# Attention among the tokens: the copy of the mixes ahead of the tile's exponential on ACT, and the division of the tokens ahead of the tile's shift on DVE

## The reference, cut to what matters

```python
slice_weights = softmax((x_mid @ W_slice + b_slice) / temp, axis=-1)
slice_norm  = slice_weights.sum(axis=2)
slice_token = einsum('bhnc,bhng->bhgc', fx_mid, slice_weights)
slice_token = slice_token / (slice_norm[..., None] + 1e-05)        # token_norm
q, k, v = slice_token @ W_q, slice_token @ W_k, slice_token @ W_v
attn = softmax(einsum('bhgc,bhkc->bhgk', q, k) * SCALE, axis=-1)
out_slice = einsum('bhgk,bhkc->bhgc', attn, v)                     # mixes
out_x = einsum('bhgc,bhng->bhnc', out_slice, slice_weights)        # product
return out_x @ W_out + b_out
```

## Time and profile before

| | us |
|---|---|
| median of 3 runs | 3429.57 (3427.73 to 3431.83) |
| the profiled execution, its own time | 3429.93 |
| span of its instructions | 3428.1 |
| PE busy in the span | 3002.8 (88%) |
| DVE, ACT, POOL busy | 2535.4, 2168.8, 1989.1 |

### The profile page before, as it was taken

The page is one execution under the profiler, slowest core; times in us unless marked ns, Lnnn a source line. Parts: engine busy times, 40 slices in busy tenths (PEclk is TensorE's granted clock), DMA queues, the critical chain, the costliest instruction groups (busy, mean ns, idle before and its releaser), DMA issues. The chain is left out here.

```text
span 3428.1 us, 66757 instructions
## 1 busy us (share of the span) xinstructions
PE 3002.8 (88%) x24922; PEld 1681.2 (49%) x24922; DVE 2535.4 (74%) x3280; ACT 2168.8 (63%) x3082; POOL 1989.1 (58%) x1191
## 2 busy tenths in 40 slices
PE   8999999969898888974699758899999999999997
PEld 6777777735555555542244323344444444444444
DVE  7888888868888888872487447776767777777773
ACT  5666666658777777751244346676766666666662
POOL 7777777712788888886100256565656565655531
PEclk9999999989999999995899879999999999999999
DMA  1111111111212212111444311111111111111102
GB/s 45 39 39 40 39 39 39 35 53 44 62 55 68 58 52 58 53 40 38 156 150 150 114 36 34 32 52 45 52 46 51 46 51 46 51 47 47 48 26 52
DMA packets 208262, 191.09 MB, mean 56 GB/s; under 512 B 76381, under 2 KB 163398, under 8 KB 207562
## 3 DMA queue, kind: packets, MB, share of 16 engines
q1 hardware_dynamic: 173850, 142.95, 14.2%
q0 software_dynamic: 25600, 26.01, 3.0%
q10 hardware_dynamic: 8496, 17.87, 1.4%
HBM read 99.08 MB, written 87.65 MB: 54 GB/s over the span
## 5 line engine op out<-in xcount | busy, mean ns | idle before, releaser
L2363 POOL TENSOR_TENSOR E_w<-E_w,E_rs 128x1024 f32<-128x1024 f32 x200 | 409.0, 2045 | 528.6 <-DVE E_rs L2271 528.6
L2356 POOL DMA_INDIRECT E_row<-yb,P_gi x400 | 391.1, 978 | 399.2 <-POOLq L93 305.4
L647 POOL DMA_INDIRECT xb<-B_yt,P_gi x400 | 523.3, 1308 | 120.8 <-issue 114.1
L203 POOL TENSOR_TENSOR A_kmask<-A_ksb,A_pack_a 128x3584 f32<-128x3584 f32 x56 | 356.5, 6365 | 151.1 <-ACT A_ksb L350 151.1
L2256 DVE TENSOR_REDUCE E_mx<-E_lg 128x16 f32<-128x1024 f32 x200 | 242.3, 1211 | 203.5 <-PE E_lg L1919 198.7
L2155 ACT ACTIVATE E_w<-E_w 128x1024 f32<-128x1024 f32 x200 | 211.5, 1057 | 281.8 <-DVE E_w L2264 238.4
L2268 DVE TENSOR_REDUCE E_sm<-E_w 128x16 f32<-128x1024 f32 x200 | 243.8, 1219 | 121.4 <-ACT E_w L2155 110.2
L1950 PEld LDWEIGHTS E_wt<-S_pack_f,E_w 128*128 128x128 f32 (+1 forms) x1600 | 173.1, 143 | 198.6 <-issue 136.3
L432 DVE COPY A_vbd<-A_v 128x512 f32<-128x512 f32 x392 | 248.6, 680 | 15.2 <-PE A_v L290 15.0
L1950 PE MATMUL E_wt<-S_pack_f,E_w 128*128 128x128 f32 (+1 forms) x1600 | 220.9, 282 | 38.5 <-ACT E_mo L2203 25.9
L2264 DVE TENSOR_TENSOR E_w<-E_lg,E_mx 128x1024 f32<-128x1024 f32 x200 | 244.8, 1224 | 6.7
(11 more groups left out here) (322 smaller groups left out, 6972.3 us busy)
## 6 DMA issues: line engine op xcount, KB each, us to landing
R_xs<-xb SPq DMA_DIRECT2D x57, 256.0 KB, 2.7
yb<-R_ys SPq DMA_DIRECT2D x57, 256.0 KB, 2.0
B_x<-h SPq DMA_DIRECT2D x25, 512.0 KB
h<-B_hh SPq DMA_DIRECT2D x25, 512.0 KB
A_xg<-in_xw SPq DMA_DIRECT2D x56, 224.0 KB, 2.9
h<-A_res ACTq DMA_DIRECT2D x56, 224.0 KB, 2.0
E_hx<-h SPq DMA_DIRECT2D x48, 256.0 KB
out<-E_ob SPq DMA_DIRECT2D x96, 128.0 KB
```

Of the source, the lines that this page charges most:

```text
L203: nc.gpsimd.tensor_tensor(kmask[i % 2][:], bc(ksb[i % 2][:].unsqueeze(2), [128, J, H, Q]), bc(head_of_row[:].unsqueeze(1).unsqueeze(3), [1 ...
L647: pool.indirect_dma_start(out=xb, out_offset=bass.IndirectOffsetOnAxis(ap=routed.gi[0:k, c, b:b + 1], axis=0), in_=yt[c % LT][0:k, D * row ...
L2356: pool.indirect_dma_start(out=row[b % LR][:, k, i], out_offset=None, in_=yb, in_offset=bass.IndirectOffsetOnAxis(ap=idx[:, c, 2 * n + i:2 ...
L2363: TT(w3, w3, bc(rs[g % 3][:].unsqueeze(2), [128, 2 * SH, G]), ALU.mult).then_inc(w_done, 1)
```

## The change

On ACT the copy of the mixes moves from behind the exponential, the roots and the table load to a place ahead of the exponential. On DVE the division of the tokens moves from behind the tile's shift to a place between `highest` and `shift`. No instruction is added or removed, and the waits go with the instructions.

```diff
@@ ACT
                     if t == 0 and logs:
                         at_block(log_in, s - 1)
                         at_block(log_out, s - 3)
+                    if step == 4:
+                        act.wait_ge(mo_done, n + 1)
+                        after(act, o_done, C * n)
+                        A(mo[:].rearrange("p b q d -> p (b q d)"), WT[:, BANK[1]], ACT.Copy).then_inc(moc_done, 1)
                     if 0 <= u < TILES:
                         exponential(u)
...
                     elif step == 3:
                         act.wait_ge(asub_done, n + 1)
                         A(at, at, ACT.Exp, scale=D ** -0.5).then_inc(aexp_done, 1)
-                    elif step == 4:
-                        act.wait_ge(mo_done, n + 1)
-                        after(act, o_done, C * n)
-                        A(mo[:].rearrange("p b q d -> p (b q d)"), WT[:, BANK[1]], ACT.Copy).then_inc(moc_done, 1)
@@ DVE
                     if 0 <= u < TILES:
                         highest(u)
+                    if step == 1:
+                        token_norm(n)
                     if begins(k) and width(k) == 1:
                         leave(k)
                     if 0 <= u < TILES:
                         shift(u)
                     if begins(k) and width(k) == 2:
                         leave(k)
-                    if step == 1:
-                        token_norm(n)
-                    elif step == 3:
+                    if step == 3:
                         scores_shift(n)
```

## The result

The changed kernel takes 3396.29 us, median of 4 runs (3393.99 to 3400.89), and the kernel before took 3428.65 us, median of 4 runs with it on the same chip. The ratio is 0.991, with a 95% interval of 0.9898 to 0.9922: faster, and by more than the 0.2% that a measurement can tell. The forecast was 3399 us, in a range of 3391 to 3413. The profiled execution of the changed kernel took 3396.83 us, 33.1 us less than that of before.

What follows compares the result with a forecast made beforehand. PE was taken to set the pace in the last part, so its idle time counts. The copy's -38.1 and the division's +7.0 us sum to -31.1, from 3429.9 to 3399 us; range 3391 to 3413.

Steps and rivals of the forecast that it cites:

- The copy of the mixes: ACT, step 4: `turn_w`'s wait of 25.9 us and 13.6 us of half clock go, 1.4 come back: -38.1 us.
- the half clock: PE, step 4, `turn_w` to `product`: clock low behind the wait; 13.6 us come back if PE doesn't stand still.
- pair 0 had its full wait and ran at 1.00: Step 4: argument against the rival that the low clock comes from the work and not the wait.
- the kind of work: Rival, step 4: transposes and 64 by 64 matmuls keep the clock low, 13.6 us stay: 3412 us; chance 0.10.
- `product`'s new wait for `leave`: PE behind step 4's `turn_w`: 0.23 us a pair in six pairs, 1.4 us given back.
- ACT did not become the bound: Rival behind step 4: `inputs` waits for `hold`, gaining 25.6 us in all there: 3411 us; chance 0.07.
- The division of the tokens: DVE, step 1: division ahead of the shift makes the shift 1.29 us late in pair 1; a loss of 7.0 us.
- The term of +7.0 us: Steps 1 and 2, seven pairs: late shift delays ACT's `keep_turned`, so PE waits at `turn_tokens`; 0.96 us in pair 1.
- The waits are split otherwise than forecast: PE, steps 1 and 2: some 0.7 us at `turn_rows`, some 1 at `turn_tokens`, none at `turn_w` for the division.
- strict FIFO order: ACT, DVE and GPSIMD don't run past a waiting instruction: the division edit costs 7.0 us; without the rule, gains 8.3.
- the things that would show it wrong: Clock of 0.5 in step 4, 1 or 2; `inputs` waiting for `hold`; or pairs 1 to 6 not some 5 us shorter.
- The forecast of 31.1 us: Whole kernel: gain from both edits, -38.1 + 7.0 us, to 3399 us; chance 0.72.

Runs made afterwards that it cites:

- the ACT edit alone: Against the kernel before, only the copy of the mixes moved ahead of the exponential, DVE as before: ratio 0.9896, 167.11 us a pair.
- the second profile of before: The unchanged kernel before, profiled once more: 1243.0 us from `tokens` of pair 0 to the end; median on this chip 3427.89 us.
- the copy behind the exponential: Against the kernel before, the copy of the mixes right behind the exponential, ahead of roots and table load, DVE as before: ratio 0.9915.
- the DVE edit with the roots first: Against the kernel before, division ahead of the shift, and in step 1 ACT's roots and table load ahead of the exponential: ratio 1.0006.
- the second execution: The changed kernel run and profiled once more, on another chip, against the kernel before: ratio 0.9924, 168.12 us a pair.
- the second one mended, and `leave` ahead: Against before: mixes' copy first, `leave` behind the exponential; step 1 weighing, division, then shift, with roots and table load ahead of the exponential: ratio 0.9874.
- the DVE edit alone: Against the kernel before, only the division of the tokens moved ahead of the shift, ACT as before: ratio 1.0047.
- the kernel with `leave` ahead: Against before, the copy of the mixes first and, in step 4, `leave` right behind the exponential, DVE as before: 3386.06 us, 166.78 a pair.

## Why the prediction was right

**The copy of the mixes.** Right, in mechanism and size. All of the wait of 25.9 us went and the half clock with it; 38.1 us were forecast and 38.7 measured in the ACT edit alone. One argument was luck: that pair 0 had its full wait and ran at 1.00 holds for that one execution. In the second profile of before the same place has the same wait, and the half clock behind it:

```profile
2215.90 1.97 PE L1950 MATMUL E_wt<-S_pack_f,E_w 128*128 128x128 f32 x8 [3.42 <-ACT E_mo L2203]
```

```profile
2215.90:2221.80 5.90, 5.90 (x17) 3.25 (x17) 0.56 (x1) 2.46 (x4) 2.75 (x3) 0.53 0.05 11
```

What rules out the kind of work is the copy behind the exponential, and the half clock costs 14.5 us in the seven pairs of that execution, where the prediction had 13.6.

`product`'s new wait for `leave` is 0.40 us and not 0.23, in five pairs and not in six: the 3.84 us in brackets are counted from the end that the profile models for PE's last matmul ahead of `turn_w`, and without the wait `turn_w` begins 0.17 us sooner than that (1.10 us behind the mixes' end, where 5.11 less 3.84 is 1.27), so PE arrives sooner at `product` and waits there for the difference. `inputs` did not wait for `hold`, so ACT did not become the bound.

**The division of the tokens.** Right in mechanism: it is a loss, and over ACT's queue, as the DVE edit with the roots first shows. The term of +7.0 us measured 7.6: 1.34 us in pair 0 and 1.05 in the others, where 1.25 and 0.96 were taken. So each pair lost 0.09 us more than the sum had; from the division's start to the shift's it is 1.11 us, where 1.10 was taken. The waits are split otherwise than forecast, in pair 1 0.50 us at `turn_rows` (some 0.7 forecast), 1.20 at `turn_tokens` (some 1) and 0.29 still at `turn_w`. DVE waited 0.22 us at the division in pair 1, with the shift queued behind it, whose maximum was done. With the Trainium skill's rule of strict FIFO order ("Perfetto Trace Analysis", section "Tensor Engine Instruction (MATMUL, LD_WEIGHTS)") the trace agrees.

**What the sum missed.** In pair 0 of the changed kernel TensorE's clock fell in step 2. The prediction named this among the things that would show it wrong, and gave it no price: a term that the sum put at nothing, and that measured 3.1 us. The timeline of the changed kernel at steps 1 and 2 of pair 0, and the window behind it:

```profile
2186.70 0.63 PE L1995 MATMUL E_wt<-S_pack_f,E_tok 128*128 128x128 f32 x4 [1.20 <-ACT E_wts L2140]
...
2189.26 2.05 PE L1888 MATMUL E_po<-E_sr,E_pack_d 128*128 128x512 f32 x2 [1.29 <-ACT E_yo L2119]
...
2191.24 1.97 PE L1894 MATMUL E_po<-E_hid,E_pack_d 64*64 64x512 f32 x2
```

```profile
2189.10:2195.90 6.80, 6.64 (x20) 2.05 (x22) 1.51 (x3) 2.73 (x5) 4.63 (x4) 0.50 0.09 14
```

PE stands still 1.20 us at `turn_tokens`, works for 1.3 us, and stands still again 1.29 us at `inputs`, which it also did before in pair 0; then the clock is 0.50. `inputs` takes 2.05 us and the next matmuls 1.97, where the trace of before has 1.10 and 1.07. From `turn_tokens` to `scores` this costs 3.1 us. In the pairs 1 to 6 `inputs` does not wait and the clock stays. With it the account of the changed kernel closes: -38.7 + 7.6 + 3.1 = -28.0 at `product` of pair 6, where its trace is 28.2 us ahead; 1.7 us are lost again behind it, where the clock is at 0.50 from 3267.7 on, and 26.4 are left.

**Right number, partly by scatter.** The forecast of 31.1 us lies between the 26 us that the two traces give for the stretch from `tokens` of pair 0 on and the 32 us of the first medians; beside the second execution the medians gave 25. The change itself is worth some 26 us in this pair of traces, five less than forecast, and those five are the half clock in pair 0 and behind pair 6.

## What to carry to other kernels

Before moving an instruction forward on an in-order engine, ask what it will wait for in its new place, and which engine lives on what is queued behind it: the copy of the mixes moved into time in which ACT waited anyway, the division moved ahead of the instruction that ACT was waiting for. A wait of PE is worth more than its length when the granted clock falls behind it, so read the clock in the stretch behind each wait. And put two edits on the chip apart: together they gave 0.991 and 168.1 us a pair, the good one alone 0.9896 and 167.1, and with the second one mended, and `leave` ahead, 0.9874 and 166.0.

## What the runs showed of the hardware that was not expected

Two short waits of PE close together were followed by the half clock in pair 0 of both profiles of the changed kernel (1.20 and 1.29 us in the first, 1.08 and 1.29 in the second), but not in pair 0 of the DVE edit alone, which has them too. In step 4 a single wait of up to 1.5 us, in the kernel with the copy behind the exponential, was never followed by it, the 3.8 us of the kernel before were each time, and so was its wait of 3.23 us in pair 6, while that of 3.42 us in pair 0 was followed by the half clock in one of two executions. The length of a wait alone doesn't tell whether the clock falls.

Behind `product` of pair 6 all ten traces have the same wait, some 1.95 us of PE at `inputs`, which ends 43.5 us after that start. In seven of them the clock falls within 2 us behind it, for 3.4 or 6.8 us; in both of before and in the kernel with `leave` ahead it stays. What decides it the runs don't show. This place is the stretch at 3267.7 in the changed kernel and at 3304.6 in the DVE edit alone, and a difference of a few us in one execution's time can be that.
